# A third of image 0's chunks added on GpSimd, and loads and stores issued in a row, in the convolution block of a four-block vision kernel

## The chip, the cores and the metric

The kernel runs on one core of a Trainium2 chip. The metric is the device time of one execution in microseconds (us).

The engines are TensorE (PE in the profile; PEld are its weight loads), VectorE (DVE), ScalarE (ACT), GpSimd (POOL) and SyncE (SP). Each has its own instruction queue and runs in its order; between engines order comes from semaphores alone. DMAs are issued from an engine's queue and carried out by 16 DMA engines.

## What is computed

The input x has 4 images of 128 channels and 96x96 pixels, float32. Two residual steps follow one another; `_gn` is a group norm over 32 groups, without scale or shift.

```python
x = x + _L0_conv_ref(_gn(x), ...)      # attention between channels
x = x + _L1_conv_ref(_gn(x), ...)      # two binarized 3x3 convolutions

# _L0: q from a wavelet transform and depthwise convolutions, k and v from 1x1 and depthwise 3x3
attn = jax.nn.softmax(jnp.einsum('bhdn,bhen->bhde', q, k) * temperature, axis=-1)
out = jnp.einsum('bhde,bhen->bhdn', attn, v).reshape(b, c, h, w)
return jnp.einsum('oc,bchw->bohw', proj_w, out)

# _L1
out = ste_sign(x)
out = conv3x3(out, bin_weight(w1))
out = batchnorm(out, gamma1, beta1)
out = ste_sign(out)
out = conv3x3(out, bin_weight(w2))
out = batchnorm(out, gamma2, beta2)
return out + identity
```

## The kernel before, in words

Four blocks run one after another, with a barrier between them. Block 1 computes group statistics and the key and value projections, block 2 the correlations of queries and keys, block 3 (`block_attention`) the softmax, which it multiplies into the output projection: one 128x128 matrix for each image, `pa_t`. Block 3 also starts two loads for block 4: the values of image 0 (into `y_first`) and x of image 0 (into `xs`), each in two halves.

The change is in block 4, `block_convolutions`. An image is 9216 pixels in the free dimension. It is cut into 24 **chunks** of 384 pixels (`CH`, four rows of the image), and these into four rounds of six (`RC`). A **piece** is one round: 128x2304 float32, 1152 KB; an image is four pieces, 4.7 MB. What happens to a chunk k of image b:

- TensorE multiplies `pa_t` with the chunk's values into one of three PSUM banks, chunk k into bank k % 3 (`project`, L1750 to L1760). Ahead of it it waits until the semaphore `s_x1` says that the chunk three before is done. The counter starts at 3 (`NBK`), so it allows the first three.
- VectorE adds x to it: x1 = x + projection, in place in `xs` (`add_x`, L1640 to L1644, one PSUM input and one SBUF input), which raises `s_x1` by one; then it takes the chunk's statistics (`x1_stats`, L1646 to L1649, `bn_stats`, one SBUF input).
- When an image is complete, VectorE combines the statistics (`aggregate`, L1658), TensorE averages over the channels of a group (`group_mean`, L1745), and VectorE forms the negative mean (`center`, L1664).
- ScalarE writes the signs of x1 minus the mean into `b4_sign`, twelve instructions for an image (L1550), TensorE runs the 3x3 convolution as nine matmuls for a chunk (`sign_conv`, L1771), ScalarE copies the result to SBUF as float16 (`copy`, L1569) and VectorE takes its statistics (`y_stats`, L1655).

Image 0's projection and adds run alone, before any convolution. Then TensorE alternates between the convolution of image b and the projection of image b + 1; the first six projections of an image stand ahead of the first convolution of the image before it. The values of images 1 to 3 come through three slots of two chunks (384 KB) from SyncE's queue (L1490 and L1498); a slot is loaded again when its two chunks are projected, so TensorE needs it four chunks later.

`xs` has room for two images. Images 0 and 2 share one half, 1 and 3 the other. GpSimd's queue does all of that traffic, in this order, and its order is that of the code: load x of image 1; store x1 of image 0 (it is read back at the end of the program); load x of image 2 once image 0's signs and statistics are done; store x1 of image 1; load x of image 3. Each load and each store is four pieces, and behind each piece the queue waits for its landing:

```python
with pool.Fori(0, RND) as r:
    piece = ds(r * (RC * CH), RC * CH)
    pool.dma_start(xs[:, b % 2, piece], d["x_c"][:, b, piece]).then_inc(s_x[b - 1], 16)
    pool.wait_ge(s_x[b - 1], r * 16 + 16)
    pool.sem_inc(s_carry, 1)
```

VectorE waits for all four pieces of an image ahead of its first add (`dve.wait_ge(s_x[b], RND * 16)`, L1700). After that come the second convolution, its batch norm, and the output; the change does not touch them.

Of the kernel before, what the change touches and what calls it, by code (L numbers as in the profile page):

```python
# [25 lines left out]
ALU = mybir.AluOpType  # L26
ACT = mybir.ActivationFunctionType
AX = mybir.AxisListType
ds = bass.ds
# [12 lines left out]
CH = ROWS * W  # L42
# [1349 lines left out]
def block_convolutions(nc, d, p):  # L1392
# [5 lines left out]
    with ExitStack() as ctx:  # L1398
# [3 lines left out]
        def sem(name):  # L1402
            return ctx.enter_context(nc.semaphore(name))

        xs = p["xs"]
# [27 lines left out]
        RC = VSLOTS * VP  # L1433
        RND = NCH // RC
        NBK = 3
        pbank = [ctx.enter_context(nc.psum_tensor(f"b4_proj_bank{i}", [C, 512], F32)) for i in range(NBK)]
        cbank = [ctx.enter_context(nc.psum_tensor(f"b4_conv_bank{i}", [C, 512], F32)) for i in range(NBK)]
        psum_g = [ctx.enter_context(nc.psum_tensor(f"b4_group_{n}", [C, 512], F32)) for n in ("mean", "var")]
# [1 line left out]
        s_c = sem("b4_constants_in")  # L1440
        s_z = sem("b4_pads_zeroed")
        s_v = [sem(f"b4_values_in{k}") for k in range(VSLOTS)]
        s_x = [sem(f"b4_x_in{b}") for b in (1, 2, 3)]
        s_xst = sem("b4_x1_stored")
        s_pm = sem("b4_proj_chunk_summed")
        s_cm = sem("b4_conv_chunk_summed")
        s_x1 = sem("b4_x1_chunk_ready")
        s_y = sem("b4_y_chunk_copied")
        s_bn = sem("b4_chunk_stats")
        s_step = sem("b4_dve_step")  # L1450
# [54 lines left out]
        @block.gpsimd  # L1505
        def _(pool):
            for k in (0, WP - 1):
                nc.gpsimd.memset(sg[:, k * WP:(k + 1) * WP], 0.0).then_inc(s_z, 1)
                nc.gpsimd.memset(padded(sg[:])[:, 1:WP - 1, k:k + 1], 0.0).then_inc(s_z, 1)

            def load_x(b):


                with pool.Fori(0, RND) as r:  # L1514
                    piece = ds(r * (RC * CH), RC * CH)
                    pool.dma_start(xs[:, b % 2, piece], d["x_c"][:, b, piece]).then_inc(s_x[b - 1], 16)
                    pool.wait_ge(s_x[b - 1], r * 16 + 16)
                    pool.sem_inc(s_carry, 1)

            load_x(1)  # L1520
            for b in range(2):
                with pool.Fori(0, RND) as r:
                    pool.wait_ge(s_x1, r * RC + (b * NCH + RC + NBK))
                    pool.sem_inc(s_carry, 1)
                    piece = ds(r * (RC * CH), RC * CH)
                    pool.dma_start(d["x1"][:, b, piece], xs[:, b, piece]).then_inc(s_xst, 16)
                    pool.wait_ge(s_xst, r * 16 + (b * RND * 16 + 16))
                    pool.sem_inc(s_carry, 1)
                pool.wait_ge(s_sg, (b + 1) * NP)
                pool.wait_ge(s_bn, X1_STATS[b])  # L1530
                load_x(b + 2)
            pool.wait_ge(s_pm, NIMG * NCH)
            for b, q in list(early) + late:
                if (b, q) in late:
                    pool.wait_ge(s_out[pieces.index((b + 2, q))], 16)
                pool.dma_start(x1_of(b, q), d["x1"][:, b, q * FQ:(q + 1) * FQ]).then_inc(s_back[b * NPC + q], 16)

        @block.scalar
        def _(act):
# [20 lines left out]
            def copy(nth, k, r=None):  # L1560
# [7 lines left out]
                    dst = y_of(b)[:, ds(r * (RC * CH) + k * CH, CH)]  # L1568
                nc.scalar.copy(dst, cbank[k % NBK][:, 0:CH]).then_inc(s_y, 1)  # L1569

            act.wait_ge(s_ready, 1)
            for r in range(NP):
                x1_sign(0, r)
# [47 lines left out]
        def _(dve):  # L1621
# [18 lines left out]
            def add_x(b, r, k):  # L1640

                dve.wait_ge(s_pm, r * RC + (b * NCH + k + 1))
                xc = xs[:, b % 2, ds(r * (RC * CH) + k * CH, CH)]
                V.tensor_tensor(xc, pbank[k % NBK][:, 0:CH], xc, ALU.add).then_inc(s_x1, 1)  # L1644

            def x1_stats(b, r, k):  # L1646
                dve.wait_ge(s_x1, r * RC + (b * NCH + k + 1 + NBK))
                V.bn_stats(bn[:, ds(r * RC + k, 1), :].rearrange("p o s -> p (o s)"),
                           xs[:, b % 2, ds(r * (RC * CH) + k * CH, CH)]).then_inc(s_bn, 1)  # L1649
# [39 lines left out]
            for half in range(2):  # L1689
                dve.wait_ge(p["s_x0"][half], 16)  # L1690
                with dve.Fori(half * RND // 2, (half + 1) * RND // 2) as r:
                    for k in range(RC):
                        add_x(0, r, k)
                        if k:
                            x1_stats(0, r, k - 1)
                    x1_stats(0, r, RC - 1)
            aggregate(0)
            center(0)
            for b in range(NIMG - 1):
                dve.wait_ge(s_x[b], RND * 16)  # L1700
                for k in range(RC):
                    add_x(b + 1, 0, k)
                    x1_stats(b + 1, 0, k)
                with dve.Fori(0, RND - 1) as r:
                    for k in range(RC):
                        add_x(b + 1, r + 1, k)
                        y_stats(b, r, k)
                        x1_stats(b + 1, r + 1, k)
                aggregate(b + 1)
                for k in range(2):  # L1710
                    y_stats(b, RND - 1, k)
                center(b + 1)
                for k in range(2, RC):
                    y_stats(b, RND - 1, k)
# [180 lines left out]
```

## Time and profile before

| | |
|---|---|
| runs | 1354.13, 1356.58, 1359.31 us; median 1356.58 |
| the profiled execution, its own time | 1358.03 us |
| its span, first to last instruction | 1356.1 us |
| TensorE busy | 1187.9 us, 88% of the span |
| VectorE, ScalarE, GpSimd busy | 1026.2, 889.0, 433.0 us |
| mean granted TensorE clock | 0.949 of full |
| block 4 | from about 895 us to the end |
| loads of x in block 4 (L1516) | 12 pieces, median 5.7 us from issue to landing |
| stores of x1 (L1526) | 8 pieces, median 5.4 us |

Shares of the whole span say little here, since the blocks have different limits. The part that is touched lies between 895 and about 1045 us, and is read by stretches and by the timeline. In a timeline row the number in brackets is the idle time of that engine before the row, and what released it. PEclk is the clock that TensorE was granted, as a share of 2.4 GHz. A projection is two matmul records (float32), a convolution of a chunk nine.

### The profile page before, as it was taken

What the parts mean: (1) busy time and instruction counts of PE and PEld (TensorE: products, weight loads), DVE (VectorE), ACT (ScalarE), POOL (GpSimd) and SP (SyncE); (2) the same over time, 40 slices, a digit from 0 to 9 for tenths busy, and PEclk for the clock granted to TensorE, in tenths of its full rate; (3) what the DMA queues carried; (4) which work ended last, traced back from release to release, by engine and by line L of the source; (5) the groups of instructions that cost most, each with busy time, mean ns of one, the idle gap of its engine ahead of it and who ended that gap; (6) DMA issues with size and microseconds to landing.
All of it is one profiled execution on the core that took longest, in us unless ns stands there. A gap on an engine that the chain in (4) does not pass through costs nothing. (4 is left out here: it accounts for less than half of the span.)

```text
span 1356.1 us, 34077 instructions
## 1 busy us (share of the span) xinstructions
PE 1187.9 (88%) x12850; PEld 935.9 (69%) x12850; DVE 1026.2 (76%) x1771; ACT 889.0 (66%) x1574; POOL 433.0 (32%) x476
## 2 busy tenths in 40 slices
PE   0899979999999999999999999888899997999800
PEld 0555568999999999999999999644455554555500
DVE  6777458999999999999999999277566733163494
ACT  0677887888888888888888886104414255666292
POOL 6200044466565556556556553100000010000010
PEclk9999989999999999999999999878989998999955
DMA  9988853553454454544444441387775230000079
GB/s 329 419 275 334 339 189 93 131 145 97 135 141 102 135 138 109 131 134 112 131 133 113 136 126 53 146 342 249 239 251 196 70 123 0 1 0 0 0 313 401
DMA packets 146920, 220.73 MB, mean 163 GB/s; under 512 B 115000, under 2 KB 116196, under 8 KB 142176
## 3 DMA queue, kind: packets, MB, share of 16 engines
q1 hardware_dynamic: 135696, 151.97, 37.2%
q0 software_dynamic: 6480, 47.19, 9.2%
q10 hardware_dynamic: 4608, 19.67, 3.7%
q8 instruction: 96, 1.57, 0.5%
q14 instruction: 40, 0.33, 0.1%
HBM read 131.58 MB, written 86.93 MB: 161 GB/s over the span
## 5 line engine op out<-in xcount | busy, mean ns | idle before, releaser
L1771 PE MATMUL b_conv_bank<-b_sign,wsign 128*128 (+1 forms) x1728 | 296.4, 328 | 10.5 <-ACT b_sign L1550 7.7
L1771 PEld LDWEIGHTS b_conv_bank<-b_sign,wsign 128*128 128x128 bf16 x1728 | 168.5, 98 | 141.5 <-issue 29.5
L824 POOL TENSOR_TENSOR b_vacc<-b_vacc 128x576 f32<-128x576 f32 x128 | 180.2, 1408 | 193.9 <-ACT b_vacc L919 193.1
L1060 PE MATMUL b_bank<-b_tkh,x_first 96*96 96x100 f16 x1536 | 220.5, 210 | 2.4 <-DVE b_tml L1041 2.4
L1062 PE MATMUL b_bank<-b_tkh,x_first 96*96 96x100 f16 x1536 | 220.2, 209 | 0.0
L1061 PE MATMUL b_bank<-b_tkl,x_first 96*96 96x100 f16 x1536 | 220.2, 209 | 0.0
L1060 PE MATMUL b_bank<-x_first,b_tmh 96*96 96x200 f16 x768 | 194.4, 253 | 15.4 <-DVE b_yl L1025 10.1
L1018 DVE SCALAR_TENSOR_TENSOR b_value_sum<-b_vin,value_taps,b_value_sum 128x576 f32<-128x576 f32 x256 | 206.3, 806 | 0.0
L1060 PEld LDWEIGHTS b_bank<-b_tkh,x_first 96*96 96x96 f16 x1536 | 192.8, 126 | 3.9 <-DVE b_tml L1041 2.7
L1062 PEld LDWEIGHTS b_bank<-b_tkh,x_first 96*96 96x96 f16 x1536 | 192.9, 126 | 0.0
L1062 PE MATMUL b_bank<-x_first,b_tml 96*96 96x200 f16 x768 | 192.8, 251 | 0.0
L1061 PEld LDWEIGHTS b_bank<-b_tkl,x_first 96*96 96x96 f16 x1536 | 191.4, 125 | 0.0
L1061 PE MATMUL b_bank<-b_yl,b_tmh 96*96 96x200 f16 x768 | 191.4, 249 | 0.0
L965 ACT CAST b_feat<-b_bank 96x400 f16<-96x400 f32 x255 | 124.4, 488 | 83.8 <-PE b_bank L1062 83.0
L919 ACT ACTIVATE b_vacc<-b_vin,value_taps 128x576 f32<-128x576 f32 x192 | 149.3, 778 | 25.2 <-POOL b_vacc L824 12.7
L753 POOL TENSOR_TENSOR b_xl<-x_first,b_xh 96x384 f16<-96x384 f32 x128 | 130.3, 1038 | 82.0 <-ACT b_xh L913 82.0
L1025 DVE TENSOR_TENSOR b_feat<-b_bank,b_feat 96x400 f16<-96x400 f32 x256 | 143.6, 561 | 8.5 <-ACT b_feat L965 6.4
L1060 PEld LDWEIGHTS b_bank<-x_first,b_tmh 96*96 96x96 f16 x768 | 93.8, 122 | 28.3 <-DVE b_yl L1025 17.1
L1025 DVE TENSOR_TENSOR b_tml<-b_bank,b_tmh 96x504 f16<-96x504 f32 (+1 forms) x155 | 99.2, 640 | 16.7 <-ACT b_tmh L965 16.7
L1655 DVE BATCH_NORM_STATS2 b_bny<-x_first (+1 forms) x96 | 53.4, 558 | 73.2 <-ACT x_first L1569 73.1
L1569 ACT CAST x_first<-b_conv_bank 128x384 f32 (+1 forms) x96 | 45.7, 479 | 90.9 <-PE b_conv_bank L1771 90.1
L1569 ACT CAST y_first<-b_conv_bank 128x384 f16<-128x384 f32 (+1 forms) x96 | 45.6, 476 | 89.1 <-PE b_conv_bank L1771 87.8
(234 smaller groups left out, 2755.1 us busy)
## 6 DMA issues: line engine op xcount, KB each, us to landing
b_vin<-value_projection_scratch SPq DMA_DIRECT2D x32, 686.0 KB, 5.6
keys_scratch<-b_khl SPq DMA_DIRECT2D x24, 784.0 KB, 5.3
value_projection_scratch<-b_vout ACTq DMA_DIRECT2D x24, 784.0 KB, 6.2
x_first<-keys_scratch SPq DMA_DIRECT2D x128, 147.0 KB, 3.0
x_first<-in_x SPq DMA_DIRECT2D x128, 144.0 KB, 5.2
values_scratch<-b_vacc SPq DMA_DIRECT2D x32, 576.0 KB, 3.5
out<-xs SPq DMA_DIRECT2D x25, 576.0 KB, 7.2
b_x<-in_x POOLq DMA_DIRECT2D x9, 1536.0 KB, 19.6
```

The costliest lines, as they stand in the source:

```text
L753: nc.gpsimd.tensor_tensor(xh[1][:, slot, im, :, :].rearrange("h c w -> h (c w)"), xraw[:, slot, im * GC * W:(im + 1) * GC * W], xh[0][:, s ...
L824: nc.gpsimd.tensor_tensor(whole, whole, room, ALU.add).then_inc(s_padd, 1)
L919: return nc.scalar.activation(out.rearrange("p (r c) -> p r c", c=W), src, ACT.Copy, scale=vtaps[:, t:t + 1])
L965: nc.scalar.copy(*target(n, 0, k)).then_inc(s_hi, 1)
L1018: nc.vector.scalar_tensor_tensor(whole if t == 8 else part, src, vtaps[:, t:t + 1], whole if t == 3 else part, ALU.mult, ALU.add).then_inc ...
L1025: nc.vector.tensor_tensor(out, src, high, ALU.subtract).then_inc(s_dve, 1)
L1060: nc.tensor.matmul(out, w_hi, m_hi, start=first, stop=False)
L1061: nc.tensor.matmul(out, w_hi, m_lo, start=False, stop=False)
L1062: return nc.tensor.matmul(out, w_lo, m_hi, start=False, stop=last)
L1569: nc.scalar.copy(dst, cbank[k % NBK][:, 0:CH]).then_inc(s_y, 1)
L1655: V.bn_stats(bny[:, ds(r * RC + (b * NCH + k), 1), :].rearrange("p o s -> p (o s)"), y_of(b)[:, ds(r * (RC * CH) + k * CH, CH)]).then_inc( ...
L1771: ins = nc.tensor.matmul(cbank[k % NBK][:, 0:CH].rearrange("p (r c) -> p r c", c=W), p["wsign"][nth // NIMG][:, t * C:(t + 1) * C], padded ...
```

## The change

Three things are changed in `block_convolutions`.

1. In image 0, chunks 2 and 5 of each round of six (`POOL_ADDS`), eight of 24, are no longer added by VectorE. ScalarE copies the projection from its PSUM bank to one of two float32 buffers (in `x_first`, unused at that time), GpSimd adds it to x in `xs`, and VectorE waits for that, raises `s_x1` in its place and takes the chunk's statistics. VectorE's order within three chunks is now two adds, their two statistics, the wait, the third statistics.
2. The four pieces of a load are issued without a wait between them, each with its own semaphore (`s_x[r]`), and so are the four pieces of a store, behind which the queue waits once for all four.
3. VectorE waits for the pieces of images 1 to 3 one by one; its rounds of these images are written out in place of a hardware loop.

```diff
--- before.py
+++ after.py
@@ -1433,6 +1433,8 @@
         RC = VSLOTS * VP
         RND = NCH // RC
         NBK = 3
+        POOL_ADDS = (2, 5)
+        summed = [p["x_first"][:, n * CH:(n + 1) * CH] for n in range(len(POOL_ADDS))]
         pbank = [ctx.enter_context(nc.psum_tensor(f"b4_proj_bank{i}", [C, 512], F32)) for i in range(NBK)]
         cbank = [ctx.enter_context(nc.psum_tensor(f"b4_conv_bank{i}", [C, 512], F32)) for i in range(NBK)]
         psum_g = [ctx.enter_context(nc.psum_tensor(f"b4_group_{n}", [C, 512], F32)) for n in ("mean", "var")]
@@ -1440,11 +1442,13 @@
         s_c = sem("b4_constants_in")
         s_z = sem("b4_pads_zeroed")
         s_v = [sem(f"b4_values_in{k}") for k in range(VSLOTS)]
-        s_x = [sem(f"b4_x_in{b}") for b in (1, 2, 3)]
+        s_x = [sem(f"b4_x_piece_in{r}") for r in range(RND)]
         s_xst = sem("b4_x1_stored")
         s_pm = sem("b4_proj_chunk_summed")
         s_cm = sem("b4_conv_chunk_summed")
         s_x1 = sem("b4_x1_chunk_ready")
+        s_px = sem("b4_proj_chunk_copied")
+        s_pa = sem("b4_x1_chunk_added_by_pool")
         s_y = sem("b4_y_chunk_copied")
         s_bn = sem("b4_chunk_stats")
         s_step = sem("b4_dve_step")
@@ -1511,21 +1515,25 @@
             def load_x(b):
 
 
-                with pool.Fori(0, RND) as r:
-                    piece = ds(r * (RC * CH), RC * CH)
-                    pool.dma_start(xs[:, b % 2, piece], d["x_c"][:, b, piece]).then_inc(s_x[b - 1], 16)
-                    pool.wait_ge(s_x[b - 1], r * 16 + 16)
-                    pool.sem_inc(s_carry, 1)
+                for r in range(RND):
+                    piece = slice(r * RC * CH, (r + 1) * RC * CH)
+                    pool.dma_start(xs[:, b % 2, piece], d["x_c"][:, b, piece]).then_inc(s_x[r], 16)
 
             load_x(1)
+            for half in range(2):
+                pool.wait_ge(p["s_x0"][half], 16)
+                with pool.Fori(half * RND // 2, (half + 1) * RND // 2) as r:
+                    for n, k in enumerate(POOL_ADDS):
+                        pool.wait_ge(s_px, r * len(POOL_ADDS) + (n + 1))
+                        xc = xs[:, 0, ds(r * (RC * CH) + k * CH, CH)]
+                        nc.gpsimd.tensor_tensor(xc, summed[n], xc, ALU.add).then_inc(s_pa, 1)
             for b in range(2):
                 with pool.Fori(0, RND) as r:
                     pool.wait_ge(s_x1, r * RC + (b * NCH + RC + NBK))
                     pool.sem_inc(s_carry, 1)
                     piece = ds(r * (RC * CH), RC * CH)
                     pool.dma_start(d["x1"][:, b, piece], xs[:, b, piece]).then_inc(s_xst, 16)
-                    pool.wait_ge(s_xst, r * 16 + (b * RND * 16 + 16))
-                    pool.sem_inc(s_carry, 1)
+                pool.wait_ge(s_xst, (b + 1) * RND * 16)
                 pool.wait_ge(s_sg, (b + 1) * NP)
                 pool.wait_ge(s_bn, X1_STATS[b])
                 load_x(b + 2)
@@ -1568,6 +1576,12 @@
                     dst = y_of(b)[:, ds(r * (RC * CH) + k * CH, CH)]
                 nc.scalar.copy(dst, cbank[k % NBK][:, 0:CH]).then_inc(s_y, 1)
 
+            act.sem_inc(s_pa, len(POOL_ADDS))
+            with act.Fori(0, RND) as r:
+                for n, k in enumerate(POOL_ADDS):
+                    act.wait_ge(s_pm, r * RC + (k + 1))
+                    act.wait_ge(s_pa, r * len(POOL_ADDS) + (n + 1))
+                    nc.scalar.copy(summed[n], pbank[k % NBK][:, 0:CH]).then_inc(s_px, 1)
             act.wait_ge(s_ready, 1)
             for r in range(NP):
                 x1_sign(0, r)
@@ -1689,19 +1703,23 @@
             for half in range(2):
                 dve.wait_ge(p["s_x0"][half], 16)
                 with dve.Fori(half * RND // 2, (half + 1) * RND // 2) as r:
-                    for k in range(RC):
-                        add_x(0, r, k)
-                        if k:
-                            x1_stats(0, r, k - 1)
-                    x1_stats(0, r, RC - 1)
+                    for n, k in enumerate(POOL_ADDS):
+                        for own in range(k - 2, k):
+                            add_x(0, r, own)
+                        for own in range(k - 2, k):
+                            x1_stats(0, r, own)
+                        dve.wait_ge(s_pa, r * len(POOL_ADDS) + (len(POOL_ADDS) + n + 1))
+                        dve.sem_inc(s_x1, 1)
+                        x1_stats(0, r, k)
             aggregate(0)
             center(0)
             for b in range(NIMG - 1):
-                dve.wait_ge(s_x[b], RND * 16)
+                dve.wait_ge(s_x[0], (b + 1) * 16)
                 for k in range(RC):
                     add_x(b + 1, 0, k)
                     x1_stats(b + 1, 0, k)
-                with dve.Fori(0, RND - 1) as r:
+                for r in range(RND - 1):
+                    dve.wait_ge(s_x[r + 1], (b + 1) * 16)
                     for k in range(RC):
                         add_x(b + 1, r + 1, k)
                         y_stats(b, r, k)
```

How the instructions stand in the queues shows at two places. The first is GpSimd's queue at the start of block 4 (`b4_x_in1` is the load of image 1, `b4_x1_chunk_ready` is `s_x1`). Before:

```order
-L1514 ISA
-L1516 REGISTER_ALU
-L1516 DMA xs<-in_x 128x2304
-L1517 ISA
-L1514 REGISTER_ALU [waits b4_x_in1]
-L1514 COMPARE_AND_BRANCH
-L1522 UNCONDITIONAL_BRANCH
-L1522 ISA
-L1526 ISA [waits b4_x1_chunk_ready]
-L1526 DMA x1_scratch<-xs 128x2304
```

Now (`b4_proj_chunk_copied` is raised by ScalarE's copy):

```order
+L1520 DMA xs<-in_x 128x2304 x4
+L1525 UNCONDITIONAL_BRANCH [waits first_image_in0]
+L1525 ISA
+L1529 ISA [waits b4_proj_chunk_copied]
+L1529 TENSOR_TENSOR xs<-x_first,xs 128x384
+L1527 REGISTER_ALU
+L1529 ISA [waits b4_proj_chunk_copied]
+L1529 TENSOR_TENSOR xs<-x_first,xs 128x384
+L1525 REGISTER_ALU
+L1525 COMPARE_AND_BRANCH
```

The four loads now stand in a row; between them and the first store are two loops of four adds, and no wait for a landing.

The second place is VectorE's queue in image 0, in the loop over rounds. Before, from the second add of a round on:

```order
-L1644 ISA [waits b4_proj_chunk_summed]
-L1644 TENSOR_TENSOR xs<-b4_proj_bank1,xs 128x384
-L1647 REGISTER_ALU
-L1648 ISA [waits b4_x1_chunk_ready]
-L1648 BN_STATS b4_bn<-xs 128x6
-L1642 REGISTER_ALU
-L1644 ISA [waits b4_proj_chunk_summed]
-L1644 TENSOR_TENSOR xs<-b4_proj_bank2,xs 128x384
```

Now, from the same add on:

```order
+L1658 ISA [waits b4_proj_chunk_summed]
+L1658 TENSOR_TENSOR xs<-b4_proj_bank1,xs 128x384
+L1661 REGISTER_ALU
+L1662 ISA [waits b4_x1_chunk_ready]
+L1662 BN_STATS b4_bn<-xs 128x6
+L1661 REGISTER_ALU
+L1662 ISA [waits b4_x1_chunk_ready]
+L1662 BN_STATS b4_bn<-xs 128x6
+L1711 ISA
+L1661 REGISTER_ALU [waits b4_x1_chunk_added_by_pool]
+L1662 ISA [waits b4_x1_chunk_ready]
+L1662 BN_STATS b4_bn<-xs 128x6
```

The add from bank 2 is gone, and in its place stands the wait for GpSimd, behind both statistics of the first two chunks.

## Rows read from the trace of the kernel before

**Rows 1.** Windows of block 4: stretch, length, busy time of each engine, PEclk, DMA, GB/s.
```profile
895.10:905.30 10.20, 9.28 (x20) 4.50 (x21) 7.05 (x15) 0.00 (x0) 1.59 (x5) 0.78 0.99 406
...
922.00:925.80 3.80, 3.80 (x8) 2.12 (x9) 1.33 (x6) 3.13 (x4) 0.00 (x0) 0.50 0.57 243
...
928.50:970.00 41.50, 41.50 (x221) 24.20 (x220) 30.75 (x62) 13.26 (x26) 2.66 (x5) 1.00 0.79 263
```

**Rows 2.** The chain that ended last, 860 to 1360 us: start, us, what.
```profile
896.09 9.20 DMA xs<-in_x
...
925.59 0.58 issue
926.19 6.28 DMA x_scratch<-xs
...
978.68 7.13 DMA xs<-in_x
```

**Rows 3.** Timeline of VectorE and of TensorE's loads: start, us, what, [idle before].
```profile
925.07 0.56 DVE L1644 TENSOR_TENSOR xs<-b_proj_bank,xs 128x384 f32<-128x384 f32 x1 [1.86 <-DMA xs<-in_x]
...
928.21 0.10 PEld L1771 LDWEIGHTS b_conv_bank<-b_sign,wsign 128*128 128x128 bf16 x1
...
985.84 0.56 DVE L1644 TENSOR_TENSOR xs<-b_proj_bank,xs 128x384 f32<-128x384 f32 x1 [6.01 <-DMA xs<-in_x]
```

**Rows 4.** TensorE at the borders of images 1, 2 and 3, timeline.
```profile
969.61 0.28 PE L1748 MATMUL b_group_mean<-b_mv,b_gmean 128*128 128x1 f32 x2
...
986.45 4.21 PE L1759 MATMUL b_proj_bank<-b_values,pa_t 128*128 128x384 f32 x6 [8.71 <-DVE xs L1644]
...
1032.15 0.28 PE L1748 MATMUL b_group_mean<-b_mv,b_gmean 128*128 128x1 f32 x2
...
1042.88 3.89 PE L1759 MATMUL b_proj_bank<-b_values,pa_t 128*128 128x384 f32 x6 [2.60 <-DVE xs L1644]
...
1087.68 0.28 PE L1748 MATMUL b_group_mean<-b_mv,b_gmean 128*128 128x1 f32 x2
```

**Rows 5.** Image 0, timeline of all engines.
```profile
899.84 0.56 DVE L1644 TENSOR_TENSOR xs<-b_proj_bank,xs 128x384 f32 x1 [0.23 <-PE b_proj_bank L1759]
...
904.69 5.07 PE L1759 MATMUL b_proj_bank<-y_first,pa_t 128*128 x12 [0.48 <-DVE xs L1644]
...
910.23 5.07 PE L1759 MATMUL b_proj_bank<-y_first,pa_t 128*128 x12 [0.47 <-DVE xs L1644]
...
920.75 0.81 DVE L1661 BATCH_NORM_AGGREGATE b_mv<-b_bn 128x2 f32<-128x144 f32 x1
...
921.73 0.50 PEld L1748 LDWEIGHTS b_group_mean<-b_mv,b_gmean 128*128 128x128 f32 x2 [4.28 <-issue]
```

**Rows 6.** Hand-overs between engines, timeline.
```profile
647.17 0.78 ACT L919 ACTIVATE b_vacc<-b_vin,value_taps 128x576 f32<-128x576 f32 x1
...
648.12 1.40 POOL L824 TENSOR_TENSOR b_vacc<-b_vacc 128x576 f32<-128x576 f32 x1 [3.87 <-ACT b_vacc L919]
...
936.20 0.35 PEld L1759 LDWEIGHTS b_proj_bank<-b_values,pa_t 128*128 128x128 f32 x2
...
937.32 0.56 DVE L1644 TENSOR_TENSOR xs<-b_proj_bank,xs 128x384 f32 x1 [0.29 <-PE b_proj_bank L1759]
...
939.44 0.56 DVE L1644 TENSOR_TENSOR xs<-b_proj_bank,xs 128x384 f32 x1 [0.63 <-PE b_proj_bank L1759]
```

**Rows 7.** Groups by form on ScalarE and GpSimd: xcount, busy us, mean ns, idle before.
```profile
L1569 ACT CAST y_first<-b_conv_bank 128x384 f32 x36 | 17.1, 478 | 63.8 <-PE b_conv_bank L1771 63.8
...
L332 POOL TENSOR_TENSOR kraw<-kraw,kscale 126x384 f32<-126x384 f32 x1 | 0.9, 893 | 0.1
```

**Rows 8.** Lines 753 (GpSimd) and 1018 (VectorE): ns min/median/max, first and last start.
```profile
L753 POOL TENSOR_TENSOR b_xl<-x_first,b_xh x128: 902/915/1437, 183.4 to 825.1; 96x384 f16<-96x384 f32 x128
...
L1018 DVE SCALAR_TENSOR_TENSOR b_value_sum<-b_vin,value_taps,b_vacc x64: 804/913/1537, 192.7 to 839.4; 128x576 f32<-128x576 f32 x64
```

**Rows 9.** Line 1490, the loads of values: from issue to landing.
```profile
DMA to landing us min/median/max: 3.1/3.6/10.9
```

## The prediction, written before the changed kernel ran

> **What bounds the kernel now.** I first read the windows of block 4 [rows 1]. Image 0's x1 (895 to 921 us) starts with the DMA engines 0.99 busy at 406 GB/s, then TensorE runs image after image at the full clock (41.50 us busy of 41.50). So once the convolutions run, TensorE sets the pace, and only what keeps it waiting is to be won. The chain that ended last [rows 2] shows one such place: from 896.1 to 978.68 + 7.13 = 985.8 us it is not TensorE but GpSimd's queue of DMAs, four loads of image 1, four stores of image 0's x1, four loads of image 2, each issued when the one before has landed. VectorE's timeline [rows 3] says what of that reaches a computing engine: two waits on loads, 1.86 and 6.01 us. The TensorE timeline at the two image borders [rows 4] gives its price: ahead of image 2 the projection stands still 8.71 us, ahead of image 3, whose pieces have landed, 2.60 us. The third place is image 0, where VectorE alone sets the pace: an add and a statistics pass for each chunk, six chunks (twelve passes) in 910.23 - 904.69 = 5.54 us, 0.46 us a pass, 2.77 us for three chunks [rows 5].
>
> **Part 1: image 0, adds on GpSimd.** Of every three chunks VectorE keeps two adds and three statistics: five passes, 2.31 us for three chunks in place of 2.77. That would win 3.2 us over the seven groups of three that follow the first. But the third chunk is now a chain. Its bank is granted to TensorE only when VectorE has counted the third chunk of the group before, because the counter rises in chunk order, and VectorE counts it only when GpSimd is done with it. One turn of this loop is:
> - GpSimd's end to VectorE's count to TensorE's weight load: 0.17. The same pattern (wait, count, weight load) is VectorE's aggregate at 920.75 + 0.81 = 921.56 and the weight load at 921.73 [rows 5].
> - Weight load to the first reader of the bank: 1.12 (936.20 to 937.32) [rows 6].
> - ScalarE's copy of 128x384 float32 out of PSUM: 0.48 [rows 7].
> - ScalarE to GpSimd: 0.17 (647.95 to 648.12) [rows 6] where no address is formed behind the wait. Here one is; the far bound is the 0.58 us that GpSimd needs ahead of its DMA [rows 2]. I take 0.25, near the row of an arithmetic instruction.
> - GpSimd's add of 384 float32: 0.90 (0.89 at 126 partitions) [rows 7].
>
> Sum 2.92 us, against 2.77 before and 2.31 of VectorE's own work: the chain is the longest, and VectorE idles about 0.6 us in every three chunks. The first group: chunk 2 is in PSUM at 899.84 [rows 5], so GpSimd ends at 899.84 + 0.48 + 0.25 + 0.90 = 901.47. Seven turns more give 921.91, and 0.65 for the hand-over and the last statistics 922.56, against 920.75 for the aggregate now: **+1.8 us**. Bounds of a turn: 2.67 (0.17 to GpSimd, and the weights loaded ahead of the count, so that the first hand-over costs nothing) gives 0.0; 3.25 (0.58 to GpSimd) gives +4.5. Below 2.67 the part wins.
>
> What could lengthen a turn is seen where GpSimd and VectorE worked side by side: GpSimd's 96x384 add took 902 ns at least, 1437 at most, and VectorE's 576-column operation with two SBUF inputs took 1.53 us instead of 0.80 [rows 8]. In image 0 VectorE's add has one input in PSUM and its statistics one input in all, so I charge nothing. The Trainium skill (SBUF — State Buffer, "SBUF: two separate sides") says the same: an exclusive lock, taken by VectorE against a reading GpSimd only with two SBUF inputs or in a two-port mode. If each of the eight adds cost the worst case instead, a turn would grow by 0.54, part 1 to +6.1, and the sum below to -1.8.
>
> ScalarE was idle through image 0 and GpSimd only waited for loads there, so the eight copies and eight adds cost nothing but the chain. GpSimd issues the four loads of image 1 ahead of its adds with nothing between them from 896.1 on, and the first copy is not done before 900.3, so the first add is not late. Its first store, in its queue behind the adds, starts near 923; now it starts at 926.19 [rows 2]. Image 0's own second half could be delayed by a deeper queue; it is needed from about 911. Until 905 the first piece of image 1 was in flight beside it anyway, and GpSimd's queue has now the same one piece at its head.
>
> **Part 2: loads of image 1.** Now they end at 925.07, after a 1.86 us wait [rows 3]. Issued together, 4.7 MB at 406 GB/s behind what is in flight land near 914 to 920, and only the first of them is waited for. The 1.86 do not all reach TensorE: from 922.0 to 925.8 its granted clock is 0.50 (1.2 GHz) [rows 1], a projection costs some 1.3 us in such a stretch (three in 3.89 us at 1042.88 [rows 4]), and three of them (from 922.1 on) fill the time until VectorE's add has freed a bank. I count: projections 3 to 5 begin at 925.5, 926.2, 926.8, convolution at 927.3 instead of 928.21 [rows 3]: **-0.9 us** (0 to -1.9).
>
> **Part 3: stores of image 0, loads of image 2.** Stores are issued together at 923 to 926, and the loads follow when all have landed and image 0's signs are read (about 934). At today's 6.3 and 7.1 us a piece, one after another, the last would land at 978; at 406 GB/s both bursts are over before 955. VectorE asks at 985.84 - 6.01 = 979.8 [rows 3]. So its wait goes. The group mean of one image to that of the next is then what it is at image 3: 1087.68 - 1032.15 = 55.53 instead of 1032.15 - 969.61 = 62.54 [rows 4]: **-7.0 us**, of which 6.1 are the wait and 0.9 the slow clock after it. What remains ahead of image 2 are 2.6 us for signs and y statistics, as at image 3. If the clock does not follow, -6.1. Image 3's load gains nothing: it landed in time.
>
> VectorE's rounds for images 1 to 3 are written out, with one wait for each piece: same work. The tail waits for nothing moved: 0.
>
> **Sum:** +1.8 - 0.9 - 7.0 = -6.1 us. The profiled execution took 1358.03 us (span 1356.1); it gives 1351.9. It was 1.45 above the median of the runs, 1356.58; against that I predict **1350.5**, or 0.45% less. What a measurement can tell from no change is about 0.5%, 6.8 us.
>
> **Rivals.**
> - *The chain is shorter than VectorE's work* (GpSimd near 0.4 us). A turn is 2.4, the aggregate starts at 900.97 + 16.8 + 0.65 = 918.4, part 1 is -2.3, sum -10.2: 1346.4. Against it stand 0.89 us for just this shape [rows 7].
> - *The turn is long*: 3.5 us by contention, or by TensorE's low clock when its work has gaps. Each add ends 0.58 later, 902.05 + 24.5 + 0.65 = 927.2; part 1 is +6.4, sum -1.5: 1355.1. For it: the lengthened adds [rows 8]. Against: at the full clock a projection is half of the 1.3 us above, so three fill two thirds of a turn and leave gaps of about 1 us.
> - *Values come late* (slower). SyncE's queue loads 384 KB of values for every two chunks, and TensorE needs them four chunks later: 4 x 2.12 (937.32 to 939.44 [rows 6]) = 8.5 us. They land in 3.6 us, 10.9 at most [rows 9]. If the queue of four pieces were served before them, a landing would take 4.7 MB / 406 GB/s = 11.6, and 3.1: 14.7 us. That is 6.2 too late in each of three bursts (stores of image 0, loads of images 2 and 3), +18.6, sum +12.5: 1369.1. It decides from a landing of 10.5 us (2.0 late, three times) on. Against it: today one GpSimd piece is in flight almost always at 263 GB/s [rows 1], and the median landing is still 3.6. The Trainium skill (DMA: Bandwidth & Descriptors, "Queues, rings and completion order") has an engine alternate between queues packet by packet, which speaks for a fair share; the landings agree.
> - *The loads do not come earlier*, because the stores' completion or the signs hold them: part 3 is 0, sum +0.9: 1357.5. The written waits leave it little room.
>
> **How the numbers follow.** Forecast 0.66, short chain 0.12, long chain 0.14, late values 0.05, no earlier loads 0.03. Within the forecast the bounds of part 1 (0.0 to +4.5) and part 3 (-6.1 or -7.0) run across the border of 6.8 us: somewhat less than half of it lies below. Faster 0.42 (0.12 of the short chain, 0.30 of the forecast), within 0.5% 0.53, slower 0.05. The range reaches from just below the short chain to just above the long one: 1346.0 to 1355.5.
>
> **What would show it.** GpSimd's adds at 0.90 us, 2.9 us apart; VectorE idle behind each third chunk, on GpSimd; aggregate near 922.5. No wait of VectorE on loads of x. Image 2's border 55.5 us ahead of image 3's. Wrong if TensorE waits for values, if adds take over 1.2 us, or if a turn differs from 2.9 by more than 0.4.

## The result, and the profile after

The changed kernel took 1360.24 us (median of 20 runs, 1357.55 to 1364.19), the kernel before 1354.91 (20 runs, 1348.21 to 1359.31): a ratio of 1.0046, interval 1.0033 to 1.0059. It is slower by half a per cent; 1350.5 was predicted, with a range of 1346.0 to 1355.5.

The profiled execution took 1358.95 us, its span is 1357.3. By stretches of block 4 (starts of TensorE's weight loads and of VectorE's aggregate):

| stretch | before | after | difference | predicted |
|---|---|---|---|---|
| first projection to aggregate of image 0 | 25.25 | 27.13 | +1.88 | +1.8 |
| to the first convolution | 7.46 | 6.54 | -0.92 | -0.9 |
| to the group mean of image 1 | 41.24 | 49.73 | +8.49 | 0 |
| group mean of image 1 to 2 | 62.54 | 54.67 | -7.87 | -7.0 |
| group mean of image 2 to 3 | 55.53 | 54.66 | -0.87 | 0 |
| to the end | 268.58 | 268.44 | -0.14 | 0 |
| sum, block 4 | 460.60 | 461.17 | +0.57 | -6.1 |

Five of the six lines lie within 0.9 us of what was predicted. The third does not, and it is the loss. TensorE's timeline there, and the chain of waits:

Timeline of TensorE in the changed kernel: start, us, line, what [idle before <- releaser].

```profile
930.12 1.64 PE L1789 MATMUL b_conv_bank<-b_sign,wsign 128*128 x9
936.69 1.65 PE L1777 MATMUL b_proj_bank<-b_values,pa_t 128*128 128x384 f32 x2 [4.92 <-DMA b_values<-values_scratch]
938.13 3.09 PE L1789 MATMUL b_conv_bank<-b_sign,wsign 128*128 x9
941.01 1.01 PE L1777 MATMUL b_proj_bank<-b_values,pa_t 128*128 128x384 f32 x2
941.86 1.64 PE L1789 MATMUL b_conv_bank<-b_sign,wsign 128*128 x9
```

The chain that ended last, 920 to 945 us: start, us, what.

```profile
927.77 8.87 DMA b_values<-values_scratch
...
936.69 1.65 PE b_proj_bank L1777 x2
938.34 2.88 PE b_conv_bank L1789 x9
```

The first convolution ends at 931.76, and the next projection, chunk 6 of image 1, begins at 936.69: its values were issued at 927.77 and landed 8.87 us later. Behind the wait TensorE runs slower: the convolution takes 3.09 us instead of 1.64. The windows show both causes, DMA engines fully busy, then a granted clock of 0.51, that is 1.2 GHz:

Windows of the changed kernel (columns as in [rows 1]):

```profile
926.00:937.00 11.00, 6.08 (x21) 3.34 (x20) 6.31 (x12) 9.43 (x12) 0.01 (x1) 0.81 1.00 383
...
937.00:941.50 4.50, 4.50 (x12) 2.21 (x12) 1.49 (x3) 0.15 (x1) 2.64 (x5) 0.51 0.93 328
```

What filled the DMA engines stands in GpSimd's timeline, four stores in a row (before: one from 926.19 on, the next after its landing [rows 2]):

GpSimd's timeline, changed kernel:

```profile
896.47 2.20 POOL L1520 DMA_DIRECT2D xs<-in_x  x4
...
922.37 0.58 POOL L1535 DMA_DIRECT2D x_scratch<-xs  x1
923.42 0.53 POOL L1535 DMA_DIRECT2D x_scratch<-xs  x1 [0.47 <-issue]
924.45 0.53 POOL L1535 DMA_DIRECT2D x_scratch<-xs  x1 [0.49 <-issue]
925.48 0.53 POOL L1535 DMA_DIRECT2D x_scratch<-xs  x1 [0.50 <-issue]
937.75 2.10 POOL L1520 DMA_DIRECT2D xs<-in_x  x4 [11.74 <-DMA x_scratch<-xs]
...
993.25 2.10 POOL L1520 DMA_DIRECT2D xs<-in_x  x4 [14.43 <-DVE b_bn L1662]
```

Values issued from 920 to 945 us landed in 8.7 to 9.1 us; in the kernel before, from 924 to 935 us, in 3.4 to 5.9:

The loads of values of the changed kernel, 920 to 945 us:

```profile
DMA to landing us min/median/max: 8.7/8.9/9.1
```

The chain of image 0 went as predicted. One turn, on all engines (answering to [rows 5, 6]):

Timeline of all engines, changed kernel:

```profile
905.20 0.30 PEld L1777 LDWEIGHTS b_proj_bank<-y_first,pa_t 128*128 128x128 f32 x2 [0.59 <-issue]
905.38 0.56 DVE L1662 BATCH_NORM_STATS2 b_bn<-xs  x1 [0.46 <-DVEq L1712]
...
906.23 0.48 ACT L1584 COPY x_first<-b_proj_bank 128x384 f32<-128x384 f32 x1 [2.41 <-PE b_proj_bank L1777]
...
906.90 1.00 POOL L1529 TENSOR_TENSOR xs<-x_first,xs 128x384 f32 x1 [1.90 <-ACT x_first L1584]
...
908.09 0.30 PEld L1777 LDWEIGHTS b_proj_bank<-y_first,pa_t 128*128 128x128 f32 x2 [0.56 <-issue]
908.28 0.56 DVE L1662 BATCH_NORM_STATS2 b_bn<-xs  x1 [0.44 <-DVEq L1712]
...
923.26 0.81 DVE L1675 BATCH_NORM_AGGREGATE b_mv<-b_bn 128x2 f32<-128x144 f32 x1
```

From one third chunk to the next, 905.38 to 908.28, it is 2.90 us: weight load to copy 1.03, copy 0.48, to GpSimd 0.19, its add 1.00, and 0.19 to the next weight load (908.09). And the image borders, where [rows 4] had 8.71 and 2.60 us: now 2.60 and 2.60.

TensorE's timeline at the borders, changed kernel:

```profile
979.70 0.28 PE L1766 MATMUL b_group_mean<-b_mv,b_gmean 128*128 128x1 f32 x2
...
990.42 3.02 PE L1777 MATMUL b_proj_bank<-b_values,pa_t 128*128 128x384 f32 x6 [2.60 <-DVE xs L1658]
...
1034.36 0.28 PE L1766 MATMUL b_group_mean<-b_mv,b_gmean 128*128 128x1 f32 x2
...
1045.09 3.02 PE L1777 MATMUL b_proj_bank<-b_values,pa_t 128*128 128x384 f32 x6 [2.60 <-DVE xs L1658]
...
1089.02 0.28 PE L1766 MATMUL b_group_mean<-b_mv,b_gmean 128*128 128x1 f32 x2
```

By these two profiles block 4 loses 0.6 us, by the medians of the runs the kernel loses 5.3. That gap is the second question: was the profiled execution of the kernel before a typical one?

### The profile page after: what moved, and what is told of

It reads as the page before. It is cut to its first block and busy times, and to the rows that moved or that the text cites. A ratio compares the mean times of both kernels' runs of the same rounds, so it can differ in the third digit from the quotient of the medians.

```text
span 1357.3 us, 33697 instructions
## 1 busy us (share of the span) xinstructions
PE 1188.4 (88%) x12850; PEld 936.7 (69%) x12850; DVE 1022.7 (75%) x1763; ACT 893.4 (66%) x1582; POOL 441.5 (33%) x484
## 5 line engine op out<-in xcount | busy, mean ns | idle before, releaser
L1789 PE MATMUL b_conv_bank<-b_sign,wsign 128*128 (+1 forms) x1728 | 297.1, 329 | 10.5 <-ACT b_sign L1558 7.7
```

What stands on the lines that cost most here:

```text
L1789: ins = nc.tensor.matmul(cbank[k % NBK][:, 0:CH].rearrange("p (r c) -> p r c", c=W), p["wsign"][nth // NIMG][:, t * C:(t + 1) * C], padded ...
```

## The experiments

Two theories. **V (values late):** the four stores in a row take the DMA engines' time just when TensorE has used up the values in its slots; 5 us of waiting, and the slow clock behind it. **P:** the loss is the adds on GpSimd, and the long wait was chance. The kernels are compared by these lengths, each read from one profiled execution: first projection to aggregate (A), group mean of image 0 to that of image 1 (G1), of 1 to 2 (G2), and the waits of TensorE for values and of VectorE for x. The times are medians, and each ratio is to runs of the kernel before that were measured beside it.

| kernel | median us | ratio to before | A | G1 | G2 | for values | for x |
|---|---|---|---|---|---|---|---|
| before, profile above | 1354.91 | | 25.25 | 47.72 | 62.54 | 0 | 7.9 |
| before_again | 1351.24 | 0.9991 [0.9971, 1.0010] | 25.26 | 47.78 | 56.84 | 0 | 2.3 |
| before_third | 1360.35, one | | 25.27 | 47.99 | 59.78 | 0 | 9.0 |
| changed | 1360.24 | 1.0046 [1.0033, 1.0059] | 27.13 | 55.29 | 54.67 | 5.7 | 0.7 |
| after_again | 1359.71 | 1.0036 [1.0014, 1.0058] | 27.00 | 55.38 | 56.14 | 5.0 | 0 |
| paced_loads | 1358.41 | 1.0040 [1.0025, 1.0054] | 26.94 | 54.68 | 54.66 | 4.5 | 0 |
| paced_stores | 1353.34 | 0.9999 [0.9983, 1.0015] | 26.78 | 48.26 | 56.19 | 0 | 0 |
| late_stores | 1353.36 | 0.9989 [0.9968, 1.0009] | 26.89 | 48.28 | 56.03 | 0.7 | 0 |
| stores_in_twos | 1352.11 | 0.9985 [0.9971, 0.9999] | 27.04 | 48.37 | 54.65 | 0 | 0 |
| bursts_only | 1351.72 | 0.9976 [0.9958, 0.9994] | 25.01 | 46.81 | 56.16 | 0 | 0 |
| load1_loads_only | 1350.60 | 0.9984 [0.9969, 0.9999] | 24.92 | 46.82 | 56.02 | 0 | 0 |
| free_bank_paced | 1350.97 | 0.9990 [0.9975, 1.0006] | 25.52 | 46.81 | 55.94 | 0 | 0 |
| six_banks_paced | 1351.17 | 0.9982 [0.9963, 1.0002] | 25.82 | 49.55 | 54.66 | 1.5 | 0 |
| six_ahead | 1348.08 | 0.9945 [0.9929, 0.9962] | 23.12 | 48.11 | 55.44 | 0.6 | 0 |

A repeats well: 25.25 to 25.27 in three executions of the kernel before, 26.78 to 27.13 in the six profiles with GpSimd's adds on three banks and their waits unchanged. G2 carries about 1.5 us of chance, since TensorE's slow stretches at image borders come and go with the same code (54.67 or 56.14 in the changed kernel).

**The changed kernel again (after_again).**

> The changed kernel unaltered, for a second profiled execution beside its own measurement. Theory V (values late): TensorE's projection waits about 5 us for the values of chunk 6 of image 1 while the four stores of image 0 are in flight, and the convolution behind it runs at half clock; from the first convolution of image 1 to its group mean 49 to 52 us (before: 41.4). Rival P (the loss is the adds on GpSimd, the long wait was chance of one execution): that stretch is near 42 us and the aggregate of image 0 is late by more than 3 us. Time against before: +5 to +6 us by both.

The stretch from the first convolution to the group mean was 48.27 us, a little under the 49 to 52 expected, and the longest wait 4.6 us: P is wrong that the wait was chance. The stretch is 1.5 us shorter than in the first profile, since the first convolution began 1.5 us later (8.09 us behind the aggregate instead of 6.54). From the first projection to the group mean of image 1 the two agree: 83.40 and 83.36 us.

**The stores one after another (paced_stores).**

```diff
                     pool.dma_start(d["x1"][:, b, piece], xs[:, b, piece]).then_inc(s_xst, 16)
+                    pool.wait_ge(s_xst, r * 16 + (b * RND * 16 + 16))
+                    pool.sem_inc(s_carry, 1)
```

> The changed kernel, but GpSimd's queue again waits behind each piece of a store. Adds on GpSimd and the loads in a row stay. Theory V: the values land in about 5 us, no wait of TensorE for them, stretch from the first convolution of image 1 to its group mean 41.5 us, that is 8.5 us less than the changed kernel: 2 to 7 us faster than before. Rival P: nothing changes, 5 us slower than before.

There is no wait for values, the stretch is 41.24 us, and the kernel is 6.4 us faster than after_again, measured beside it. From the first projection to the group mean of image 1 it is 76.02 us, 7.3 less than in after_again. V holds, P falls: the adds are the same. But the kernel is as fast as before, not 2 to 7 us faster. Values now land so:

paced_stores, loads of values from 924 to 935 us:

```profile
DMA to landing us min/median/max: 3.8/4.3/4.8
```

**The stores in a row, but later (late_stores).**

```diff
             for b in range(2):
+                if b == 0:
+                    pool.wait_ge(s_pm, NCH + 2 * RC)
                 with pool.Fori(0, RND) as r:
```

> The changed kernel, but the four stores of image 0, still in a row, begin only when TensorE has projected 12 chunks of image 1, behind the start of the image where six projections stand in a row. Theory V with the start of the image as the cause (a slot is needed about 4 us after its reload there, 8.5 us later in the alternation): landings of 9 us, but waits of under 1 us each; stretch to the group mean under 44 us, 1 to 6 us faster than before unless the loads of image 2 now come late. Rival Q (a queue of four pieces starves TensorE at any place): the same wait of some 5 us, only later, and time as the changed kernel. Rival P: as the changed kernel.

The burst begins at 946.19, and the values issued in it land as late as 9.3 us, in the median 5.7. Yet TensorE waits 0.7 us in all:

late_stores: loads of values from 945 to 965 us, then the waits of TensorE in block 4 (us, times, longest).

```profile
DMA to landing us min/median/max: 3.2/5.7/9.3
...
PE b_proj_bank L1779 <- DMA b_values<-values_scratch: 0.7, 1, 0.7
```

That wait is the landing of 9.3 less the 8.5 us after which a slot is needed in the alternation. So a burst costs time only where a slot is needed soon: 4.0 us after its reload at the start of an image (927.77 to 931.76), where the first six projections have emptied all slots, 8.5 in the alternation. That any burst in the alternation costs as much as the first one falls with it.

The kernel before has no slack there either. In before_again the values asked for from 924 to 935 us landed in 4.6 to 7.1 us, and TensorE's weight load for chunk 6 of image 1 had to wait a little:

before_again, timeline of TensorE's weight loads:

```profile
931.48 0.30 PEld L1759 LDWEIGHTS b_proj_bank<-b_values,pa_t 128*128 128x128 f32 x2 [0.26 <-DMA b_values<-values_scratch]
```

**Two stores at a time (stores_in_twos).** The rounds of the store are written out, with this in them:

```diff
+                for r in range(RND):
+                    if r == 2:
+                        pool.wait_ge(s_xst, (b * RND + 2) * 16)
```

> The changed kernel with one more wait: GpSimd's queue issues two pieces of a store, waits for both, then the other two. Theory V by the number of stores ahead (each takes its share of the time): values land in 5.5 to 8 us, wait of TensorE 1 to 4 us, stretch to the group mean 42 to 47 us, between paced_stores and the changed kernel. Rival (two in a row already fill the DMA engines, and those two are done before the values count): wait as in the changed kernel, 5 us, 48 us; or none, 41.2.

The first two stores are issued at 921.1 and have landed by 929.1, when the other two are issued; the values are asked for from 926.7 on. Two of these loads land in 3.6 and 3.7 us, one in 8.6, which was not waited for. The expected wait of 1 to 4 us did not come; the stretch is 41.24 us. That is the second alternative of the rival (no wait). The run doesn't tell what two stores in flight cost for the whole of a load.

**The loads of images 2 and 3 one after another, stores in a row (paced_loads).** In `load_x` a wait follows each piece for b > 1.

> The changed kernel, but the loads of images 2 and 3 wait behind each piece again; the stores stay in a row. Theory V: only the burst of stores does the harm and only the order of things, not the loads' burst, brings image 2 in time: same 5 us wait for values and the same time as the changed kernel within 2 us, no wait for x of image 2. Rival (the burst of loads shares in the harm at 938 to 957 us): 2 us or more faster than the changed kernel.

1358.41 us and a wait of 4.5: as the changed kernel. The burst of loads has hardly a share in the harm: the changed kernel has a second wait for values in it, 0.75 us at 956.96 (0.40 in after_again), which is gone here, and the medians don't show it. It isn't needed for the gain either. With paced loads the first load of image 2 is issued at 937.7 and the last at 956.8 (before: 955.3 and 978.7), so x is in time without it. Most of these 17.6 us come from the stores in a row, which took 15.5 us from the first issue to that load instead of 29.1; 4.0 come from the first store's earlier issue (922.2 instead of 926.2).

**Without adds on GpSimd (bursts_only, load1_loads_only).** Both give VectorE's loop of image 0 back as it was; the second also paces the stores.

> The changed kernel without its adds on GpSimd: VectorE adds all chunks of image 0 as before; loads and stores still in a row, and since no add stands between them the stores of image 0 go out piece by piece from about 905 us on. Theory V: these stores are mostly done before the values are reloaded at 925 us, so little wait; aggregate of image 0 at 25.3 us from the first projection instead of 27.1; 6 to 10 us faster than before. Rival Q: the wait stays, same as before or slower. Rival P: all of the loss goes, about 8 us faster than before, so P and V agree here, and only paced_stores tells them apart.

> No adds on GpSimd, stores paced by a wait behind each piece, loads in a row. Against paced_stores this takes away the adds alone (and lets the stores begin at about 905 us). Theory V and the chain of 2.9 us: aggregate at 25.3 us from the first projection instead of 26.8, first convolution 41.2 us ahead of the group mean, no wait for values; 1 to 2 us faster than paced_stores, as fast as bursts_only within 1 us. Rival (a queue in a row does something useful beside the waits): slower than bursts_only by 2 us or more.

Both are faster than before, as both theories said; that no value is waited for is what V said. bursts_only issues its stores between 902.8 and 919.3 us, and the values asked for from 925.3 us on land in 3.2 to 3.7. Against paced_stores, load1_loads_only has its aggregate 1.86 us earlier (24.92 against 26.78), and from the aggregate to the first convolution it needs 6.55 us instead of 8.00. The second part is TensorE's clock. The six projections (twelve matmul records) take 7.05 us in paced_stores, whose windows have a granted clock of 0.50 from 926 to 932 us, and 5.67 in the changed kernel's first profile (0.85 from 926 to 932 us):

Timeline of TensorE, paced_stores, then (second fence) the changed kernel:

```profile
926.17 7.05 PE L1779 MATMUL b_proj_bank<-b_values,pa_t 128*128 128x384 f32 x12
```

```profile
924.62 5.67 PE L1777 MATMUL b_proj_bank<-b_values,pa_t 128*128 128x384 f32 x12
```

The long form (8.00 to 8.11 us from the aggregate to the first convolution) stands in five of the six profiles that have the changed kernel's adds as they are, the short one (6.54) in its first profile alone; bursts_only, load1_loads_only and free_bank_paced have 6.55. So these adds cost 1.9 us ahead of the aggregate and mostly another 1.5 behind it. What makes the clock rise sooner or later there, no run shows. The two kernels' times come from different comparisons (0.9984 and 0.9999 of before, intervals that touch). bursts_only won 3.2 us, less than the 6 to 10 expected. The missing part is the next point.

**The kernel before, twice more (before_again, before_third).**

> The kernel before, unaltered, for a second profiled execution. All runs so far were about 3 us slower against it in measured time than their profiled block 4 said (span less the first projection: 460.6 us for the profiled execution of before, 461.2 and 465.0 for the changed kernel, 453.9 for bursts_only). If the first profiled execution of before was a long one: block 4 near 457 us, with VectorE's wait for image 2's load under 4 us instead of 6. If not: 460 to 461 again, and the missing 3 us lie ahead of block 4.

> The kernel before once more, one look. The first profiled execution had VectorE wait 6.0 us for image 2's load, the second under 2. If the load chain of twelve pieces varies from execution to execution with its landings, the wait is again between 0.5 and 3 us and block 4 (span less the first projection) 454 to 457 us; if the first was the rule, 6 us and 460.

VectorE's waits for x of images 1 to 3:

Waits of VectorE, before_again, then (second fence) before_third: us in total, times, longest.

```profile
DVE xs L1644 <- DMA xs<-in_x: 2.3, 2, 1.4
```

```profile
DVE xs L1644 <- DMA xs<-in_x: 9.0, 3, 3.9
```

The load chain of the kernel before has its wait in every execution, but of very different size: 7.9, 2.3 and 9.0 us in all, of which 6.01, 1.44 and 3.91 stand ahead of image 2. The executions took 1358.03, 1353.23 and 1360.35 us. So the first profiled execution was a long one; for the third 0.5 to 3 us had been expected, and that was wrong too. Twelve pieces follow one another there, each 5 to 9 us; what they sum to decides. The medians of the kernel before, 1351.24 to 1354.94, lie nearer to the short execution, and its runs spread over 11.1 us (1348.21 to 1359.31), those of load1_loads_only over 5.1. So what the earlier loads win is 7 us in some executions and under 1 (G2 56.84 to 56.0) in others.

**The bank given back by ScalarE's copy (free_bank_paced).** TensorE's projection of a GpSimd chunk waits for `s_px`, the copy, and no longer for the add.

> paced_stores, but TensorE's projection into the bank of a GpSimd chunk waits for ScalarE's copy alone and not for GpSimd's add. If the chain TensorE, ScalarE, GpSimd, VectorE is what makes three chunks cost 2.9 us: VectorE's own five passes bound it then, 2.3 to 2.5 us for three chunks, aggregate 3 to 4 us earlier than paced_stores (23.0 to 23.8 us from the first projection), time 3 to 4 us less. Rival (GpSimd's add slows VectorE or is itself the pace): 2.7 us or more for three chunks, 1 us or less won.

The aggregate comes 1.3 us earlier, where 3 to 4 were expected (25.52 against 26.78), and the first convolution another 1.45 (6.55 against 8.00 us behind the aggregate). VectorE still idles 0.80 us, but only once in two groups of three: 5.51 us for six chunks, 2.76 a turn.

free_bank_paced, timeline of VectorE and of TensorE:

```profile
906.28 0.56 DVE L1665 BATCH_NORM_STATS2 b_bn<-xs  x1 [0.81 <-DVEq L1715]
...
911.79 0.56 DVE L1665 BATCH_NORM_STATS2 b_bn<-xs  x1 [0.80 <-DVEq L1715]
...
907.44 4.50 PE L1783 MATMUL b_proj_bank<-y_first,pa_t 128*128 x12 [1.02 <-DVE xs L1661]
```

TensorE's idle time ahead of 907.44 is for VectorE's add. In TensorE's order the projection of the third chunk stands behind that of the second, whose bank VectorE's add of the group before gives back. One link was cut, and the queue's order seems to be the next; the kernel six_ahead below tests it.

**Six banks (six_banks_paced, six_ahead).** Image 0's projections also use the three banks of the convolution, idle then.

> paced_stores, but image 0's projections go through six PSUM banks (the three of the convolution stand idle then), so that TensorE may be six chunks ahead and neither GpSimd's add nor the order of projections holds the next ones back. If the chain through the banks sets the turn of 2.9 us (2.76 where only ScalarE's copy was waited for): VectorE's five passes set it now, 2.3 to 2.4 us for three chunks, aggregate 22.8 to 23.8 us from the first projection against 26.8, about 3 us less time than paced_stores and 1 to 2 us less than load1_loads_only. Rival (GpSimd and VectorE slow one another, or the add on GpSimd is the pace): 2.7 us or more for three chunks.

This missed too: 5.52 us for six chunks. In it the first three projections of a round wait for chunk 3 of the round before, so TensorE was not six ahead there. And though its stores go one by one, TensorE waited 1.2 us for the values of chunk 6 of image 1: the place has no slack with other kernels either (six_ahead: 0.6). With the rounds written out and the wait at six:

```diff
+            return (pbank + cbank)[k] if b == 0 else pbank[k % NBK]
...
+                if b == 0:
+                    if r * RC + k >= 2 * NBK:
+                        pe.wait_ge(s_x1, r * RC + k + 1 - NBK)
```

> six_banks_paced with the wait put right: there the first three projections of a round waited for chunk 3 of the round before, so TensorE was only three ahead at the start of each round and GpSimd's adds came 2.6 and 0.9 us after its last. Here image 0's projections are written out and each waits for the chunk six before. If the chain through the banks is what sets the turn: 2.3 to 2.4 us for three chunks, aggregate 22.8 to 23.8 us from the first projection (six_banks_paced 25.8), 2 to 3 us less time than six_banks_paced. Rival (something else paces GpSimd): 2.7 us again, same time.

six_ahead, VectorE's timeline:

```profile
906.33 1.00 DVE L1663 TENSOR_TENSOR xs<-b_conv_bank,xs 128x384 f32 x2
907.25 1.47 DVE L1667 BATCH_NORM_STATS2 b_bn<-xs  x3
908.63 1.00 DVE L1663 TENSOR_TENSOR xs<-b_proj_bank,xs 128x384 f32 x2
909.56 1.47 DVE L1667 BATCH_NORM_STATS2 b_bn<-xs  x3
...
917.98 0.80 DVE L1680 BATCH_NORM_AGGREGATE b_mv<-b_bn 128x2 f32<-128x144 f32 x1
```

2.30 us for three chunks (906.33 to 908.63), VectorE without a gap, the aggregate at 23.12 us. This version is faster than both kernels: 1348.08 us, 0.9945 of before [0.9929, 0.9962]. It has the adds on GpSimd, the loads in a row, and the stores one by one. So the chain through the banks, and not the add on GpSimd, held the turn at 2.90 us.

## Why the prediction was wrong

- **The chain of image 0: right.** 2.92 us a turn predicted, 2.90 found; part 1 +1.8, found +1.88. Single terms were off and cancelled: GpSimd's add 1.00 instead of 0.90, the weight load to the reader 1.03 instead of 1.12, ScalarE to GpSimd 0.19 instead of 0.25. That the chain, not VectorE, sets the turn is shown by six_ahead.
- **Start of the convolutions: right for the loads, by luck for the changed kernel.** -0.9 was predicted, and -0.92 found in this profile. The kernels without GpSimd's adds have it: 6.55 us from the aggregate, against 7.38 to 7.73 in three executions of the kernel before. But in after_again, paced_loads, paced_stores, late_stores and stores_in_twos, which all have the changed kernel's adds, it is 8.00 to 8.11 us, +0.5 to +0.7 instead of -0.9; paced_stores has its granted clock of 0.50 there. The sum had no term for that.
- **"4 x 2.12 (...) = 8.5 us" in the rival of late values: the step that failed.** "TensorE needs them four chunks later" holds in the alternation of projection and convolution, and late_stores shows it. At the start of an image six projections stand in a row; chunk 6 is asked for 4.0 us after the reload (927.77 to 931.76). A landing over 4.0 us costs time there, and not one from 10.5 on; 8.9 were measured, so that the chance of 0.05 was far too little. Its price was wrong in the other direction: one burst counts, not three, and costs 5 us of wait and 2 to 3 of slow clock. The sum had no term for it at all, and it was worth +6.4 us by the medians of after_again and paced_stores, +7.3 by their profiles. Rows of the kernel before bore on it: landings of up to 10.9 us [rows 9]. "TensorE waits for values" stood among the prediction's own signs of being wrong, and it is the one that came.
- **"-7.0 us" for image 2: mis-sized.** Right in this pair of profiles (-7.87), wrong as a difference of medians. It was read from one execution, whose wait of 6.01 us is no property of the kernel; the two others had 1.44 and 3.91 us there. paced_stores, which has all terms of the forecast but the stores in a row, stands at 0.9999 of before: its gain at the loads and its loss of 1.5 us at the adds and some 0.5 at the first convolution cancel. An estimate from these numbers: of the 11.4 us between the forecast (-6.1) and the medians (+5.3), 6.4 are the stores in a row and about 1.5 the late start, and the rest of 3.5 is gain at the loads that the typical execution of the kernel before doesn't leave to be won.
- **Stores and loads "issued together" (parts 2 and 3):** the sum takes the pieces in a row for a gain only, since the queue's own waits go. The waits also kept the DMA engines free for another queue.

## What to carry to other kernels

A wait between two DMAs in a queue is also a limit on what is in flight; before it is taken away, look which other queue's transfer is needed soonest, and take its slack where the consumer's work is densest, not on average. A wait that stands in one profiled execution and ends on a chain of many transfers can have a wide spread; a second profiled execution tells whether the gain is there as a rule. And an operation handed to another engine inside a ring of few buffers can lose: here it was 2.77 us for three chunks without it, 2.90 with it and three banks, 2.76 with six banks but TensorE not six ahead, and 2.30 with six banks and TensorE six ahead. What the queues wait for counts as much as the number of buffers.

## What the runs showed of the hardware

- A load of 384 KB lands in 8.9 us (median; 7.4 to 10.0 over the changed kernel, after_again and paced_loads) beside four stores of 1152 KB in a row, in 4.3 (paced_stores) beside stores one by one, at 1.00 and 0.86 (932 to 938 us) of the DMA engines' time. The first three loads of values, beside image 1's four pieces in a row, took up to 18.9 us (before 10.9); nobody waited for them.
- A wait of 4.9 us of TensorE is followed by 4.5 us at a granted clock of 0.51, and a convolution of 3.09 us instead of 1.64.
- GpSimd's add of 128x384 float32 took 0.99 to 1.00 us in all eight cases of the changed kernel, in seven with VectorE's statistics beside it (906.90 beside 906.83). In six_ahead VectorE's adds with an input in PSUM ran beside it too, and it took the same: the add below overlaps those from 906.33 us on, and one at 899.87 us, with VectorE idle, took 0.99. That neither lengthens it is what the Trainium skill says (SBUF — State Buffer, "SBUF: two separate sides").

six_ahead, GpSimd's timeline:

```profile
905.82 1.00 POOL L1532 TENSOR_TENSOR xs<-x_first,xs 128x384 f32 x1 [0.91 <-ACT x_first L1589]
```
